# Gated cross-attention and low-rank linear layer: the context rows of three batches prepared in two passes instead of three

## The reference, cut to what matters

```python
def reference(x, ctx_1024, g_xattn, g_ffn, W, b, lora_down, lora_up, down_aux, up_aux):
    # x (4, 2048, 512), ctx_1024 (4, 77, 512), W (512, 512), all float32
    def _L0_xattn_ref(h, v):
        scores = jnp.einsum('bsd,bvd->bsv', h, v)
        probs = jax.nn.softmax(scores, axis=-1)
        return jnp.einsum('bsv,bvd->bsd', probs, v)
    def _L0_ffn_ref(h, W, b, lora_down, lora_up, down_aux, up_aux):
        lilora_weight = up_aux @ (lora_up @ (lora_down @ down_aux))
        base = jnp.einsum('bsi,oi->bso', h, W) + b
        return base + jnp.einsum('bsi,oi->bso', h, lilora_weight)
    x = x + jnp.tanh(g_xattn[0]) * _L0_xattn_ref(_layernorm(x), ctx_1024)
    x = x + jnp.tanh(g_ffn[0]) * _L0_ffn_ref(_layernorm(x), W, b, lora_down, lora_up, down_aux, up_aux)
    return x
```

## Time and profile before

| | |
|---|---|
| median of 3 runs | 311.59 us (311.43 to 312.00) |
| profiled execution, its own time | 311.45 us |
| its span | 309.6 us |
| instructions | 6482 |
| ScalarE busy | 187.3 us, 61% |
| VectorE busy | 235.3 us, 76% |
| GpSimd busy | 226.3 us, 73% |
| DMA, mean | 182 GB/s |

### The profile page before, as it was taken

One profiled execution on the slowest core, in us unless ns is written; L12 is line 12 of the kernel. 1 busy time (PEld: TensorE's weight loads), 2 busy tenths in 40 slices (PEclk: granted clock), 3 DMA queues, 4 the chain that ended last, 5 costly groups with the idle time before them and its releaser, 6 DMA issues.

```text
span 309.6 us, 6482 instructions
## 1 busy us (share of the span) xinstructions
PE 300.9 (97%) x2086; PEld 285.4 (92%) x2086; DVE 235.3 (76%) x743; ACT 187.3 (61%) x546; POOL 226.3 (73%) x276
## 2 busy tenths in 40 slices
PE   6999999999999999999999999999999999999992
PEld 4689999998999999998999999999899999999992
DVE  3977877885887787797588777798587887777765
ACT  2856655663676666656476656656476656566552
POOL 3767778786588777777577787778488777877763
PEclk9999999999999999999999999999999999999999
DMA  7763654344695454455394465554097554444013
GB/s 211 261 233 139 213 212 159 137 179 147 223 270 186 166 186 169 171 203 206 110 270 193 164 227 203 205 194 178 38 288 243 204 205 168 175 159 176 22 55 136
DMA packets 16470, 56.39 MB, mean 182 GB/s; under 512 B 1985, under 2 KB 1985, under 8 KB 16436
## 3 DMA queue, kind: packets, MB, share of 16 engines
q1 hardware_dynamic: 15856, 54.65, 51.3%
q10 hardware_dynamic: 580, 1.32, 1.1%
HBM read 35.84 MB, written 16.78 MB: 170 GB/s over the span
## 4 chain that ended last, share of the span: by engine, by line
PE 95%; DMA 1%; DVE 1%; ACT 1%; issue 0%; POOLq 0%; POOL 0%; ACTq 0%; DVEq 0%
PE y_ps L555 66%; PE y_ps L586 10%; PE a_ps L581 10%; PE c_ps L531 3%; PE y_ps L563 2%; DMA low_in_sb<-in_low_in 1%; PE y_ps L626 1%; PE a_ps L513 1%; PE y_ps L631 1%; PE a_ps L543 1%; PE c_ps L522 0%; PE a_ps L547 0%; PE y_ps L647 0%; PE y_ps L508 0%; DVE o_sb L753 0%
## 5 line engine op out<-in xcount | busy, mean ns | idle before, releaser
L555 PE MATMUL y_ps<-wc,xT 128*128 128x334 f32 (+1 forms) x1536 | 228.2, 302 | 0.0
L555 PEld LDWEIGHTS y_ps<-wc,xT 128*128 128x128 f32 x1536 | 214.4, 189 | 2.0
L336 POOL TENSOR_TENSOR x_bias<-x,bias_g 128x512 f32<-128x512 f32 x63 | 81.3, 1290 | 63.2 <-DVE x L715 63.2
L324 POOL TENSOR_TENSOR xT<-xt_raw,xT 128x512 fp32r<-128x512 f32 x64 | 83.1, 1298 | 0.1
L424 ACT ACTIVATE expd<-y_ps,neg_max,rs 128x77 f32<-128x77 f32 x64 | 26.7, 417 | 80.2 <-DVE neg_max L705 80.2
L438 ACT ACTIVATE squares<-x,x_nmean 128x512 f32<-128x512 f32 x64 | 46.4, 725 | 16.5 <-DVE x_nmean L723 16.5
L352 POOL TENSOR_TENSOR rs<-stat_eps,half_neg 128x2 f32<-128x2 f32 (+1 forms) x67 | 46.1, 688 | 5.2
L753 DVE SCALAR_TENSOR_TENSOR o_sb<-y_ps,rs,x_bias 128x512 f32<-128x512 f32 x64 | 48.0, 750 | 1.4 <-issue 0.8
L586 PEld LDWEIGHTS y_ps<-stacks,pT 109*128 109x128 f32 (+1 forms) x256 | 39.8, 191 | 5.4
L715 DVE SCALAR_TENSOR_TENSOR x<-a_ps,x_sb 128x512 f32<-128x512 f32 x64 | 43.7, 683 | 0.2 <-PE a_ps L581 0.2
L694 DVE BATCH_NORM_STATS2 bn<-x_sb 128x6 f32<-128x512 f32 x64 | 43.8, 684 | 0.0
(11 more groups left out here) (80 smaller groups left out, 191.7 us busy)
## 6 DMA issues: line engine op xcount, KB each, us to landing
x_sb<-in_x SPq DMA_DIRECT2D x32, 512.0 KB, 4.3
xt_raw<-in_xt SPq DMA_DIRECT2D x31, 512.0 KB, 5.2
out<-o_sb SPq DMA_DIRECT2D x31, 512.0 KB, 3.0
stacks<-v_hi SPq DMA_DIRECT2D x3, 308.0 KB
stacks<-v_hi SPq DMA_DIRECT2D x3, 256.0 KB
stacks<-v_lo SPq DMA_DIRECT2D x3, 256.0 KB
w_all<-in_w ACTq DMA_DIRECT2D x2, 256.0 KB, 6.3
xt_raw<-in_xt ACTq DMA_DIRECT2D x1, 512.0 KB, 7.1
```

Source lines behind the costliest of these rows:

```text
L324: pool.tensor_tensor(xT[:, k % TRING, 1, :, :], xt_raw[:, k % XRING // UNIT, k % UNIT, :, :], xT[:, k % TRING, 0, :, :].bitcast(F32), ALU. ...
L336: pool.tensor_tensor(x1_bias[:, q, :], x1[:, j, :], bias_g[:, :], ALU.add).then_inc(x1b_ready, 1)
L555: mm = pe.matmul(y_half(k, h)[:, 0:n], xT[:, k % TRING, part, c, :], wc[:, c, w, h * H:h * H + n], start=(c == 0 and part == 0 and w == 0) ...
```

## The change

The 3 x 77 = 231 context rows of batches 1 to 3 lie one behind another in memory. They are now prepared in two passes: the first, in batch 0, takes 125 rows (the 77 of batch 1 and the first 48 of batch 2), the second, in batch 1, takes 106 (the last 29 of batch 2 and the 77 of batch 3). In batch 2 and 3 nothing is prepared. The buffers of a pass grow from 77 to 128 partitions, `ct` gets two slots of 128 rows, and the PSUM view of the turned rows gets a stride of 128. The instructions of a pass stay the same in number; their widths follow `PACK[n]`.

The context load is issued in two pieces, the second with what is left over a multiple of 16 rows (112 + 13, 96 + 10). The copies into `stacks` of batch 1 stand where they stood. Those of batch 2 come in two parts: three "head" copies at the second unit of batch 1, and six "rest" copies at the seventh unit of batch 1, behind both casts of the second pass. Those of batch 3 are issued at the second unit of batch 2. `ctx_columns(2)` takes the columns of batch 2 from both slots of `ct`, in four copies; the other batches have two as before.

The diff, cut to its core (in the other places that it touches `V` becomes `PACK[n]`, and `ct[:, part]` becomes `ct_part(n, part)`):

```diff
+    TAIL = 48
+    PACK = (V, V + TAIL, 2 * V - TAIL)
+    BY = 16
...
-        c_rows = sb("c_rows", [V, D])
-        ct = sb("ct", [P, 2, KC, V], F32R)
+        c_rows = sb("c_rows", [P, D])
...
+        ct = sb("ct", [P, 2, 2, KC, P], F32R)
+        v_hi = sb("v_hi", [P, 2 * D], F32R)
+        v_lo = sb("v_lo", [P, 2 * D], F32R)
...
-        ct_ps = c_ps[:, 0:KC * V].rearrange("p (c v) -> p c v", c=KC)
...
+        ct_all = c_ps[:, :].rearrange("p (c v) -> p c v", c=KC)
+        def ct_ps(n):
+            return ct_all[:, :, 0:PACK[n]]
+        def ct_part(n, part):
+            return ct[:, n % 2, part, :, 0:PACK[n]]
...
-            return a_ps[0:V, :] if n == 0 else c_ps[0:V, :]
+            return a_ps[0:V, :] if n == 0 else c_ps[0:PACK[n], :]
...
-                if t % TB >= HB and t < T - TB:
+                if t % TB >= HB and t < T - 2 * TB:
                     prep(t // TB + 1, t % TB)
...
+        def packs(t, k):
+            return t % TB == k and t < T - 2 * TB
+        def columns_done(n):
+            return 2 * n + 2 + (2 if n >= 2 else 0)
...
-            return 16 * (DMAS * (n // 2 + 1) + (FIRST - DMAS if n % 2 == 0 else 0))
+            return 16 * (FIRST, DMAS, FIRST + 3 + DMAS + 1, 2 * DMAS)[n]
...
             def load_ctx(n):
-                sp.dma_start(c_rows[:, :], ctx_in[n:n + 1].rearrange("o v d -> (o v) d")).then_inc(ld_ctx, 16)
...
+                at = V + (n - 1) * PACK[1]
+                cut = PACK[n] // BY * BY
+                for a, z in ((0, cut), (cut, PACK[n])):
+                    sp.dma_start(c_rows[a:z, :], ctx_in.rearrange("b v d -> (b v) d")[at + a:at + z, :])\
+                        .then_inc(ld_ctx, 16)
...
+            def copy(n, rows, s, source, at, cols):
+                sp.dma_start(stacks[rows, n % 2, s, cols].bitcast(F32),
+                             source[at:at + rows.stop - rows.start, cols].bitcast(F32)).then_inc(stacked[n % 2], 16)
+            def stack_hi(n, at, cols):
+                copy(n, slice(0, V), 0, v_hi, at, cols)
+                copy(n, slice(96, K0), 0, v_hi, at + Q, cols)
+                copy(n, slice(0, Q), 1, v_hi, at, cols)
+            def stack_lo(n, at, cols):
+                copy(n, slice(V, V + R), 0, v_lo, at + Q, cols)
+                copy(n, slice(Q, P), 1, v_lo, at, cols)
+            def stack_head(n):
+                both = slice(0, 2 * D)
+                copy(n, slice(0, TAIL), 0, v_hi, V, both)
+                copy(n, slice(0, TAIL), 1, v_hi, V, both)
+                copy(n, slice(Q, Q + TAIL), 1, v_lo, V, both)
+            def stack_rest(n):
+                both = slice(0, 2 * D)
+                copy(n, slice(TAIL, Q), 0, v_hi, 0, both)
+                copy(n, slice(Q, V), 0, v_hi, Q - TAIL, both)
+                copy(n, slice(96, K0), 0, v_hi, Q - TAIL, both)
+                copy(n, slice(TAIL, Q), 1, v_hi, 0, both)
+                copy(n, slice(V, V + R), 0, v_lo, Q - TAIL, both)
+                copy(n, slice(Q + TAIL, P), 1, v_lo, 0, both)
...
-            def stack(n):
-                if n < 2:
-                    sp.wait_ge(zeroed, 1)
-                else:
-                    sp.wait_ge(y_ready, TB * (n - 1))
+            def rows_cast(n):
                 sp.wait_ge(v_hi_ok, 2 * n + 1)
-                stack_hi(n, slice(0, 2 * D))
                 sp.wait_ge(v_lo_ok, 2 * n + 2)
-                stack_lo(n, slice(0, 2 * D))
...
-                if n < B - 1:
-                    if k == 1:
-                        sp.wait_ge(v_lo_ok, 2 * n + 2)
-                        load_ctx(n + 1)
-                    if k == NU - 2:
-                        stack(n + 1)
+                if n < 2 and k == 1:
+                    sp.wait_ge(v_lo_ok, 2 * n + 2)
+                    load_ctx(n + 1)
+                if n == 0 and k == NU - 2:
+                    rows_cast(1)
+                    stack_hi(1, 0, slice(0, 2 * D))
+                    stack_lo(1, 0, slice(0, 2 * D))
+                if n == 1 and k == 1:
+                    sp.wait_ge(y_ready, TB)
+                    stack_head(2)
+                if n == 1 and k == NU - 2:
+                    rows_cast(2)
+                    stack_rest(2)
+                if n == 2 and k == 1:
+                    sp.wait_ge(y_ready, 2 * TB)
+                    stack_hi(3, V - TAIL, slice(0, 2 * D))
+                    stack_lo(3, V - TAIL, slice(0, 2 * D))
                 unit(u)
...
                 for part in range(2):
-                    pool.tensor_copy(wc[:, :, part, D:D + V], ct[:, part, :, :].bitcast(F32)).then_inc(c_cols, 1)
+                    pool.tensor_copy(wc[:, :, part, D:D + V], ct_part(0, part).bitcast(F32)).then_inc(c_cols, 1)
...
-                act.wait_ge(ld_ctx, 16 * n + 16)
...
+                act.wait_ge(ld_ctx, 32 * n + 16)
...
                     act.wait_ge(stacked[(n - 1) % 2], stack_landed(n - 1))
-                act.activation(v_hi[:, 0:D], c_rows[:, :], ACT.Copy, scale=tg[0:V, 0:1]).then_inc(v_hi_ok, 1)
+                if n == 2:
+                    act.wait_ge(stacked[0], 16 * (FIRST + 3))
+                act.activation(v_hi[0:PACK[n], 0:D], c_rows[0:PACK[n], :], ACT.Copy, scale=tg[0:PACK[n], 0:1]).then_inc(v_hi_ok, 1)
...
                     act.wait_ge(c_tr, n + 1)
-                    act.activation(ct[:, 0, :, :], ct_ps, ACT.Copy).then_inc(ct_hi_ok, 1)
+                    act.activation(ct_part(n, 0), ct_ps(n), ACT.Copy).then_inc(ct_hi_ok, 1)
 
             def ctx_columns(n):
 
                 act.wait_ge(s_ready, TB * n)
-                act.wait_ge(ct_lo_ok, n + 1)
+                act.wait_ge(ct_lo_ok, min(n, 2) + 1)
                 for part in range(2):
-                    act.activation(wc[:, :, part, D:D + V], ct[:, part, :, :].bitcast(F32), ACT.Copy).then_inc(c_cols, 1)
+                    if n == 2:
+                        act.activation(wc[:, :, part, D:D + TAIL], ct[:, 1, part, :, V:V + TAIL].bitcast(F32), ACT.Copy)\
+                            .then_inc(c_cols, 1)
+                        act.activation(wc[:, :, part, D + TAIL:D + V], ct[:, 0, part, :, 0:V - TAIL].bitcast(F32), ACT.Copy)\
+                            .then_inc(c_cols, 1)
+                    else:
+                        at = 0 if n == 1 else V - TAIL
+                        act.activation(wc[:, :, part, D:D + V], ct[:, n % 2 if n == 1 else 0, part, :, at:at + V].bitcast(F32),
+                                       ACT.Copy).then_inc(c_cols, 1)
...
-                if switches(t, STATS):
+                if packs(t, STATS):
                     ctx_rows_hi(t // TB + 1)
-                if switches(t, TAKE):
+                if packs(t, TAKE):
                     ctx_product_hi(t // TB + 1)
...
-                        mm = pe.transpose(ct_ps[:, c, :], c_cent[:, c * P:(c + 1) * P], ident[0:V, 0:V])
+                        mm = pe.transpose(ct_ps(n)[:, c, :], c_cent[0:PACK[n], c * P:(c + 1) * P], ident[0:PACK[n], 0:PACK[n]])
...
-                            mm = pe.matmul(cw_ps(n), ct[:, lhs, c, :], wc[:, c, rhs, 0:D],
+                            mm = pe.matmul(cw_ps(n), ct_part(n, lhs)[:, c, :], wc[:, c, rhs, 0:D],
...
-                        pe.wait_ge(c_cols, 2 * (t // TB) + 2)
+                        pe.wait_ge(c_cols, columns_done(t // TB))
```

More of the change, by code:

```diff
@@ L39, in build_kernel @@
     FIRST = DMAS + 1
-    assert TB == 2 * HB and V + R <= 96 and D == 512
+    TAIL = 48
+    PACK = (V, V + TAIL, 2 * V - TAIL)
+    BY = 16
+    assert TB == 2 * HB and V + R <= 96 and D == 512 and B == 4 and TAIL % BY == 0 and V <= PACK[2] <= PACK[1] <= P
     x_units = x.rearrange("b (u p n) d -> (b u) p n d", p=P, n=UNIT)
@@ L74, in build_kernel @@
         wc = sb("wc", [P, KC, 2, D + VP], F32R)
-        c_rows = sb("c_rows", [V, D])
-        c_bn = sb("c_bn", [V, 6])
-        c_mv = sb("c_mv", [V, 2])
-        c_cent = sb("c_cent", [V, D])
-        ct = sb("ct", [P, 2, KC, V], F32R)
-        v_hi = sb("v_hi", [V, 2 * D], F32R)
-        v_lo = sb("v_lo", [V, 2 * D], F32R)
+        c_rows = sb("c_rows", [P, D])
+        c_bn = sb("c_bn", [P, 6])
+        c_mv = sb("c_mv", [P, 2])
+        c_cent = sb("c_cent", [P, D])
+        ct = sb("ct", [P, 2, 2, KC, P], F32R)
+        v_hi = sb("v_hi", [P, 2 * D], F32R)
+        v_lo = sb("v_lo", [P, 2 * D], F32R)
         stacks = sb("stacks", [P, 2, 2, 2 * D], F32R)
@@ L271, in _ @@
             sp.wait_ge(v_hi_ok, 1)
-            stack_hi(0, slice(0, D))
+            stack_hi(0, 0, slice(0, D))
             sp.wait_ge(ld_x[0], 16)
@@ L276, in _ @@
             sp.wait_ge(v_lo_ok, 1)
-            stack_lo(0, slice(0, D))
+            stack_lo(0, 0, slice(0, D))
             first_stack_lo()
@@ L369, in _ @@
         def _(act):
-            act.dma_start(c_rows[:, :], ctx_in[0]).then_inc(ld_ctx, 16)
+            act.dma_start(c_rows[0:V, :], ctx_in[0]).then_inc(ld_ctx, 16)
             act.dma_start(low_out_sb[:, :], low_out).then_inc(ld_out, 16)
@@ L542, in first_product @@
```

(20 more changed lines are left out.)

6 lines of the change are left out of this document (3 added, 3 removed).

## The result

The changed kernel takes 308.30 us, the median of 4 runs (308.16 to 308.53), against 311.79 us before (4 runs, 311.43 to 314.36, beside it on the same chip). On a second chip it was 308.45 against 312.02, 0.9876 (0.9842 to 0.9911). The forecast was 308.8 us with a range of 308.3 to 309.5, made from 311.59 for the kernel before: a gain of 2.8 us, 3.3 at most. The time stands on the range's lower edge, and the gain against the kernel beside it is 3.5 us, outside the range. The direction was right and so were the terms for the pass that goes; what failed is the step that took the spacing of all unchanged matmuls as given ("4.33 everywhere after"), and a smaller one on VectorE.

The account below looks back on a forecast made before the run. TensorE was taken to bound the kernel, its chain without gaps: 311.45 − 3.10 (pass) + 0.26 (transposes) + 0.05 (weights) = 308.66, plus 0.14 for the median gives 308.8 us, range 308.3 to 309.5.

Parts of the forecast that it names:

- The pass that goes: Three preparations become two; TensorE loses one pass's transposes (0.31) and context product (2.79): −3.10 us.
- 4.33 everywhere after: Distances between L581s outside the two passes, first of batch 2 included, were to stay at 4.33 us.
- Wider transposes: Passes' transposes on TensorE, moving operand from 77 columns to 125 and 106: +0.26 us, ends 0 and +0.34.
- Wider weights: Context product on TensorE, weights from 77 columns to 125 and 106: +0.05 us, upper end +0.82 with loads' growth uncovered.
- Rival (a): TensorE's weight loads and transposes dearer than the nearest rows, +0.82 and +0.34: 309.65 us; chance 0.06.
- Column copies: Four copies before batch 2 on ScalarE in place of two: +0.20 us there, covered by 0.43, so cost 0.
- rival (b): Tile 31's probabilities late behind four copies at the old ones' price, TensorE waits 0.3: 309.1 us; chance 0.05.
- SyncE's queue: Moved context loads and stack copies, six issues at unit 14 ending at 160.0: cost 0, at worst 0.7 us.
- rival (c): Batch 2's stack lands after 167.87 and TensorE's first product there waits; 309.5 us at the rows' worst; chance 0.03.
- Rival (d): Saving doesn't appear because something beside TensorE paces batch 2 once the pass is gone: 311.6 us; chance 0.02.
- one each of ScalarE's and VectorE's instructions of a pass; they stand beside TensorE and give nothing: ScalarE's and VectorE's instructions that go with the dropped pass were to change the time by nothing.

Follow-up runs that it names:

- no_third: Kernel before without its third preparation, batch 3 computed with batch 2's context; stretch from first to last L581 276.56 us, −2.77.
- third_back: Changed kernel with TensorE's part of a third pass put back into batch 2, result unused; 311.40 us, +3.24 us in the stretch.
- layout: Kernel before with only the larger context buffers and PSUM stride 128, three passes of 77 rows kept; stretch 0.89 us shorter, tiles 4.3132 us apart.
- pad_gap448: after_pad with a gap of 448 bytes behind ct; 307.37 us, ratio 0.9831 to the kernel before.
- after_pad: Changed kernel with seven one-element memsets added on VectorE in the middle of batch 2; 308.19 us, stretch 0.28 us shorter.

## Why the prediction was wrong, and what of it held

**The pass that goes**: right. no_third gives −2.77 with the stop's 0.30 in it, third_back +3.24; forecast was 3.10.

**Wider transposes**: right, 0.43 and 0.36 for 0.43 and 0.37. In the distances of their tiles the two together cost 0.20 more than before, not 0.26: behind the narrow ones the next three matmuls took 0.51 us (layout), behind the wide ones 0.47 or 0.48. The interpolation between 68 ns at 77 columns and 110 at 128 held at both new widths.

**Wider weights**: the forecast of 0.05 for both passes was near; it is 0.01 a pass at most: 2.77 at 77 columns (layout), 2.78 at 125 and 2.78 at 106. That holds for this placement; in pad_gap448 the product takes 2.84 at 125 columns and 2.77 at 106. The weight load itself became longer, as the forecast's upper end had feared; the groups of the changed kernel show it, beside the 145 ns of the earlier trace rows, and at most 0.01 us a pass of it reaches the chain:

```profile
L589 PEld LDWEIGHTS c_ps<-wc,ct 128*125 128x125 f32 x12 | 2.2, 185 | 0.5
L589 PEld LDWEIGHTS c_ps<-wc,ct 128*106 128x106 f32 x12 | 2.0, 170 | 0.6
```

Rival (a) falls. The Trainium skill's rule ("TensorE: Matmul & The Clock Gate", "The mechanism") that a weight load overlaps matmuls in flight only in other row groups does not hold here: 24 longer loads added 0.01 us a pass at most, where the estimate by the page's columns/1.2 was 0.77 us in all. The same section also lets a load go ahead into a background weight buffer, and the trace agrees with that.

**Column copies**: the forecast of no cost was right, and rival (b) did not come. The four copies take 0.91 us to the exponential (0.92 forecast), the probabilities end at 160.77 + 0.41 = 161.18 and the weight load of their transpose comes at 161.41, without a wait.

```profile
158.94 0.36 ACT L453 ACTIVATE wc<-ct 128x192 fp32r<-128x192 f32 x1 [0.41 <-PE y_ps L613]
159.21 0.29 ACT L455 ACTIVATE wc<-ct 128x116 fp32r<-128x116 f32 x1
...
159.85 0.40 ACT L482 ACTIVATE expd<-y_ps,neg_max,rs 128x77 f32<-128x77 f32 x1
...
160.77 0.41 ACT L489 ACTIVATE p_ext<-expd,e_inv 128x154 f32<-128x154 f32 x1
```

**SyncE's queue**: right again, and rival (c) did not come: the first distance of batch 2 is an ordinary one. The six copies are issued from 155.34 to 160.02 (forecast 160.0) and the next store at 160.21, where it was 160.07 before. The price of an issue was right as well, 0.81 us for the first four against 0.82.

```profile
155.34 3.23 SPq L248 DMA_DIRECT2D stacks<-v_hi  x4
...
158.63 1.39 SPq L248 DMA_DIRECT2D stacks<-v_lo  x2
...
160.21 0.43 SPq L294 DMA_DIRECT2D out<-o_sb  x1
```

**Rival (d)** falls with no_third, where the pass gives its 3.10 and the stop alone takes from it.

**What failed** is a step that the sum put at nothing without a reason. "4.33 everywhere after" took the spacing of unchanged matmuls as given, and the change's larger buffers as free. They are not: the tiles came 12.7 ns closer, 61 times in the loop, −0.77 us, and the two products that are left 0.05 shorter where +0.05 was forecast; layout shows both without the change. In the other direction "one each of ScalarE's and VectorE's instructions of a pass; they stand beside TensorE and give nothing" had the count wrong (VectorE executes 737 instructions where it had 743, and one waiting instruction less) and missed that these seven shift a stop of its stream onto the last tiles, +0.30 us (no_third, after_pad). All taken from distances, the stretch is −3.10 (the pass) + 0.20 (transposes) − 0.05 (products) + 0.30 (the stop) − 0.77 (spacing) = −3.42, as measured; the forecast for the same stretch was −2.79. It was luck that the two missing terms have opposite signs: with the spacing alone the time would have been about 308.0. The range was too narrow, since a few nanoseconds on each of the loop's matmuls had no bound in it.

**Open.** Why the spacing depends on where buffers lie is not settled. Shown is that it repeats at one pair of numbers that agree within 2048 bytes (82880 and 89024). A period of 256, 512 or 1024 bytes could do as well, or a longer one that divides the 6144 bytes between them; 128 and less can't, since 82848 and 88608, and 82880 and 88640, agree within 128 bytes and differ in spacing. Nor is it shown which buffers count: everything behind ct moved together, and only wc and the context buffers were moved against it. What the other engines and the transfers read and write in the moved buffers at the same time was not varied; the context product, whose operands stayed, makes them a rival to TensorE's own two reads. Other remainders weren't tried, so a better one than pad_gap448's may exist.

## What to carry to other kernels

When one engine's chain has no gap, take its distances from the chain, remove and add pieces at their own price, and the sum holds to 0.1 us; here every term of the pass on TensorE did. Where a change moves or resizes on-chip buffers, run the old kernel with only the new sizes beside it before the rest is explained or credited; 0.8 of the 3.4 us here are due to that alone, and 32 bytes of gap in the old kernel give 2.0 in the stretch, without any of the change. A small stop that repeats through a profile is harmless until its place coincides with the tail: look there first when instruction counts change on any engine.

## What the runs showed of the hardware that I had not expected

- The spacing of matmuls depends on where buffers lie in a partition: 4.295 to 4.327 us for the same 31 matmuls, 0.7%, at a granted clock of 1.00, reproducible to 1 ns a matmul, and the same for the same number of bytes from wc to xT. It changed even for matmuls whose own operands had not moved (the context product: 2.80, 2.78 and 2.75 us). The Trainium skill, "TensorE: Matmul & The Clock Gate", "Step-by-step: what each phase is for", says "Loading the next tile's weights doesn't steal SBUF read bandwidth from the running matmul". No run here tells whether that holds: what collides was not isolated.
- VectorE stops, with nothing awaited that the profile names, at places of its instruction stream that lie about a multiple of 128 apart. Counted in the traces, stops of 0.29 to 0.32 us come behind instruction 63 in all thirteen profiles, behind 832 in those with 1001 instructions and behind 960 in those with 994. Smaller ones come behind 449 or 705 and are not constant: behind 449 it is 0.15 us before and in no_third, 0.06 in the changed kernel and 0.09 in after_pad. All these counts leave 63 to 65 when divided by 128, and all stand ahead of an output (L753), which waits for several semaphores; behind 192, 320 and 576, where other instructions stand, none shows. Why VectorE stops there is not shown.
